# Two-layer gated attention and feed-forward on one core: second norm's transposes moved ahead of the second score pair, first values moved up, layer 1's norm scale and offset behind the transposes

## Chip, cores and metric

One core of a Trainium2 chip runs the kernel. The metric is device microseconds for one execution. All arithmetic is fp32; where a product needs more than one pass of rounded operands, it is split into a high and a low part.

## What is computed

The batch has 8 sequences of 256 tokens, 256 wide. Each of two layers adds a gated cross attention (16 heads, 77 context rows) and a gated feed-forward. Layer 0's feed-forward has 8 experts by position; layer 1's has one shared expert and 7 routed ones with room for 732 tokens each. Only layer 1's second norm has a scale and an offset (`ln_g`, `ln_b`).

```python
x = x + tanh(g_xattn[0]) * attention0(layernorm(x), ctx)
x = x + tanh(g_ffn[0])   * experts_by_position(layernorm(x))
x = x + tanh(g_xattn[1]) * attention1(layernorm(x), ctx)
h = layernorm(x) * ln_g + ln_b
logits = h @ Wr                       # top 2 of 7 experts
x = x + tanh(g_ffn[1])   * (routed(h, logits) + silu(h @ W1s) * (h @ W3s) @ W2s)
```

## The kernel before

It is written by hand for each engine; every engine runs its own instruction list in order, and semaphores join them. There are four stages: attention of layer 0 (to about 150 us), layer 0's experts (to 250), attention of layer 1 (to about 400), and the shared and routed experts of layer 1.

Attention runs one batch element per step, `attention_step` in each engine's block, software-pipelined over three steps. The heads are four units u = 0..3: units 0 and 1 are the first half of the columns (dt 0) for both halves of the rows, units 2 and 3 the second (dt 1). In step g TensorE (PE) computes the scores of g (`scores`, L562, two pairs), transposes the probabilities (`prob_transposes`, L573), multiplies with the values of g-1 (`weighted_values`, L582, dt 0 and dt 1), transposes the attention output of g-2 (`out_transposes`, L523 from `o_q`), projects it (`project_out`, L594), transposes the first norm of g+1 (`norm_t`, L523 from `xn`), makes its queries (`queries`, L602), and transposes the second norm of g-3 (`norm2_t`, L523 from `xn2`, which the profile also prints as `xn`). In layer 1 it adds the router's logits of g-3 (`route_logits`, L551).

PSUM sets the order. `bank[0]` takes, one after the other, the second norm's, the output's and the first norm's transposes and the queries; each must be copied out by ScalarE (ACT) before the next is written: `norm2_t` copies to `stage` (L982), `out_t` to `o_t` (L1012, two instructions), `norm_t` to `xn_t` (L975), `queries` to `q_t` (L991). `bank[1]` takes values, projection and, in its last columns, the logits. VectorE (DVE) takes the maxima and subtracts them (`max_sub`), normalises the values (`normalise_out`, L1345 and L1347), adds the projection to the residual (`add_attention`, L1355), and makes both norms; GpSimd (POOL) makes the reciprocal roots and the low parts. In layer 1 the second norm is made in two DVE steps, `centre2` (L1312, with `ln_g`) and `norm2` (L1326, with `ln_b`), from full rows of scale and offset.

SyncE (SP) issues all loads. Per step it places the values of one batch element on the block diagonal tile `v_blk`, 8 small DMAs for each half (`place_values`, L335). Half dt of g is placed once `weighted_values(g-1, dt)` has read the old contents:

```python
if not isinstance(g, int) or g > 0:
    sp.wait_ge(pv_psum, KT * g - KT + 1 + dt)
```

In layer 0 a step also zeroes a part of two tensors in device memory (L344, L345).

In the routed experts PE transposes the next expert's rows in the middle and at the end of an expert (`slots_t`, L874); ACT copies them to the high part (`slots_hi`, L1221), DVE makes the low part (`slots_lo`, L1593).

## Time and profile before

| | us |
|---|---|
| median of 3 runs | 887.07 (884.72 to 891.02) |
| the profiled execution | 888.85 |
| its span, first to last instruction | 887.10 |
| PE busy | 851.7 (96% of the span) |
| DVE, ACT, POOL busy | 525.6, 427.2, 275.7 |
| mean granted TensorE clock | 0.981 of full |

Span and durations come from the one profiled execution. Its time stands 1.75 us above its span and 1.78 us above the median. A busy PE is not a PE at its peak, since matmuls overlap; how long a piece takes is read from the start of one to the start of the next. Rows that print x20 for ten products count both passes of an fp32 product.

### The profile page before, as it was taken

Reading aid. Unit: us, or ns where it says so; the run is one execution under the profiler, and the core shown is the slowest. Engines: PE = TensorE matmul, PEld = TensorE weight load, DVE = VectorE, ACT = ScalarE, POOL = GpSimd, SP = SyncE. Lnnn points to the kernel's source line nnn. Section 1 sums busy time; section 2 is a strip of 40 time slices with the busy share of each in tenths; the row PEclk is TensorE's granted clock in tenths of the full one; section 3 lists DMA queues with packets and bytes.
Section 4 is the critical chain, followed back from the end, with each engine's and each line's share of the span. In section 5 each row is a group of like instructions: output and inputs, shape, how many; then the busy total and the mean of one; then the engine's idle time right before and its main releaser. Section 6 shows DMA issues by size and latency. Waiting matters only on the chain.

```text
span 887.1 us, 18253 instructions
## 1 busy us (share of the span) xinstructions
PE 851.7 (96%) x6116; PEld 799.5 (90%) x6116; DVE 525.6 (59%) x1128; ACT 427.2 (48%) x939; POOL 275.7 (31%) x328
## 2 busy tenths in 40 slices
PE   8899989999969999999999999999999999999997
PEld 6788878999948888879898999999999999999986
DVE  4677744555567887647336573636556473645648
ACT  3556654777736665632324462615345361525431
POOL 5244314877754443135552002020100102020130
PEclk9999989999969999999999999999999999999999
DMA  5242327766530000020213323413233131422152
GB/s 204 66 132 95 124 67 278 219 218 211 180 101 5 8 6 6 8 96 19 70 45 98 104 74 84 125 40 108 80 95 86 64 106 52 130 74 96 62 185 101
DMA packets 74841, 86.98 MB, mean 98 GB/s; under 512 B 31188, under 2 KB 46962, under 8 KB 74668
## 3 DMA queue, kind: packets, MB, share of 16 engines
q1 hardware_dynamic: 70956, 79.86, 29.3%
q0 software_dynamic: 3552, 6.55, 2.2%
q8 instruction: 24, 0.39, 0.2%
q14 instruction: 21, 0.17, 0.1%
q10 hardware_dynamic: 288, 0.01, 0.0%
HBM read 64.08 MB, written 23.63 MB: 99 GB/s over the span
## 4 chain that ended last, share of the span: by engine, by line
PE 80%; SPq 9%; DVE 4%; issue 3%; ACT 2%; DMA 1%; POOL 0%; DVEq 0%; ACTq 0%; POOLq 0%
PE score L274 14%; PE score L276 14%; PE score L275 13%; SPq L335 8%; PE bank_p L274 7%; PE bank_p L275 7%; PE bank_p L276 7%; PE bank L582 5%; PE bank L594 2%; PE bank L602 2%; PE bank_p L573 2%; PE bank L523 2%; PE bank L874 1%; PE score L562 1%; DVE residual L1734 1%
## 5 line engine op out<-in xcount | busy, mean ns | idle before, releaser
L1135 ACT ACTIVATE silu<-score 128x366 f32<-128x366 f32 (+1 forms) x144 | 72.6, 504 | 278.5 <-PE score L276 278.5
L1494 DVE TENSOR_TENSOR prod<-silu,score 128x366 f32<-128x366 f32 (+1 forms) x144 | 82.1, 570 | 114.8 <-ACT silu L1135 112.5
L274 PE MATMUL score<-xe_hi,w_hi 128*128 128x366 f32 x448 | 149.3, 333 | 0.0
L276 PE MATMUL score<-xe_hi,w_lo 128*128 128x366 f32 x448 | 148.3, 331 | 0.0
L275 PE MATMUL score<-xe_lo,w_hi 128*128 128x366 f32 x448 | 148.2, 331 | 0.0
L1979 POOL DMA_INDIRECT slots_out<-yh,home_of x42 | 40.8, 972 | 336.7 <-DVE yh L1621 336.7
L274 PE MATMUL bank_p<-w_hi,hid_hi 128*122 128x256 f32 (+1 forms) x448 | 127.3, 284 | 0.7 <-DVE hid_lo L1502 0.5
L275 PE MATMUL bank_p<-w_lo,hid_hi 128*122 128x256 f32 (+1 forms) x448 | 125.7, 281 | 0.0
L276 PE MATMUL bank_p<-w_hi,hid_lo 128*122 128x256 f32 (+1 forms) x448 | 125.6, 280 | 0.0
L1805 POOL TENSOR_TENSOR w_lo<-raw,w_hi 128x512 fp32r<-128x512 f32 x62 | 82.6, 1363 | 31.3 <-ACT w_hi L949 24.3
L582 PE MATMUL bank<-v_blk,prob_t 128*128 128x136 f32 x640 | 84.4, 290 | 5.6 <-DMA v_blk<-values 5.2
L274 PE MATMUL score<-act_hi,w_hi 128*128 (+2 forms) x256 | 86.8, 339 | 0.0
L582 PEld LDWEIGHTS bank<-v_blk,prob_t 128*128 128x128 f32 x640 | 80.3, 198 | 6.8 <-issue 6.1
L276 PE MATMUL score<-act_hi,w_lo 128*128 (+2 forms) x256 | 86.1, 336 | 0.0
L275 PE MATMUL score<-act_lo,w_hi 128*128 (+2 forms) x256 | 85.9, 336 | 0.0
L274 PEld LDWEIGHTS score<-xe_hi,w_hi 128*128 128x128 f32 x448 | 84.6, 189 | 0.2 <-issue 0.2
L276 PEld LDWEIGHTS score<-xe_hi,w_lo 128*128 128x128 f32 x448 | 84.7, 189 | 0.0
L275 PEld LDWEIGHTS score<-xe_lo,w_hi 128*128 128x128 f32 x448 | 84.6, 189 | 0.0
L274 PEld LDWEIGHTS bank_p<-w_hi,hid_hi 128*122 128x122 f32 (+1 forms) x448 | 82.6, 184 | 1.7 <-DVE hid_lo L1502 0.9
L275 PEld LDWEIGHTS bank_p<-w_lo,hid_hi 128*122 128x122 f32 (+1 forms) x448 | 82.7, 185 | 0.1
L276 PEld LDWEIGHTS bank_p<-w_hi,hid_lo 128*122 128x122 f32 (+1 forms) x448 | 82.7, 185 | 0.0
L1502 DVE TENSOR_TENSOR hid_lo<-prod,hid_hi 128x366 fp32r<-128x366 f32 (+1 forms) x136 | 76.2, 560 | 0.5 <-ACT hid_hi L1185 0.3
(208 smaller groups left out, 1723.0 us busy)
## 6 DMA issues: line engine op xcount, KB each, us to landing
raw<-w_second_d SPq DMA_DIRECT2D x108, 256.0 KB, 2.7
raw<-w_first_d SPq DMA_DIRECT2D x72, 256.0 KB, 3.1
slot_rows<-yh SPq DMA_DIRECT2D x8, 771.0 KB, 3.4
yh<-slot_rows SPq DMA_DIRECT2D x8, 674.6 KB
v_blk<-values SPq DMA_DIRECT2D x256, 5.0 KB, 2.0
slots_out<-yh SPq DMA_DIRECT2D x8, 512.0 KB, 4.3
wa<-attn_w_d SPq DMA_DIRECT2D x8, 256.0 KB, 4.2
yh<-slots_out SPq DMA_DIRECT2D x4, 512.0 KB, 7.9
```

The source lines that it names most:

```text
L274: nc.tensor.matmul(o, a_hi, b_hi, start=start, stop=False)
L275: nc.tensor.matmul(o, a_hi, b_lo, start=False, stop=False)
L276: return nc.tensor.matmul(o, a_lo, b_hi, start=False, stop=stop)
L335: sp.dma_start(v_blk[h:P:HT, dt * PT:(dt + 1) * PT, h * HD:(h + 1) * HD], v_g[:, at:at + HD].rearrange("(t k) d -> k t d", t=PT)).then_inc ...
L523: last = nc.tensor.transpose(o[:, kt * S + h * P:kt * S + (h + 1) * P], src[:, h, kt * P:(kt + 1) * P], ident[:])
L573: last = nc.tensor.transpose(bank_p[grp][:, i * P:(i + 1) * P], prob[u][:, j * P:(j + 1) * P], ident[:])
L582: last = nc.tensor.matmul(bank[1][:, qt * VW:(qt + 1) * VW], prob_t[:, dt * PT + j, qt * P:(qt + 1) * P], v_blk[:, dt * PT + j, :], start= ...
L1135: nc.scalar.activation(silu[0:rows_n, buf, 0:width], src, ACT.Silu).then_inc(silu_done, 1)
L1494: nc.vector.tensor_tensor(prod[0:rows_n, buf, 0:width], silu[0:rows_n, buf, 0:width], up, ALU.mult).then_inc(gu_free, 1)
L1502: nc.vector.tensor_tensor(lo, prod[0:rows_n, buf, 0:hi.shape[-1]], hi.bitcast(F32), ALU.subtract).then_inc(hid_ready, 1)
L1805: return nc.gpsimd.tensor_tensor(w_lo[:, at, :], raw[:, slot_f, :], w_hi[:, at, :].bitcast(F32), ALU.subtract)
L1979: nc.gpsimd.indirect_dma_start(out=ye, out_offset=bass.IndirectOffsetOnAxis(ap=home_of[:, e, j:j + 1], axis=0), in_=y_out[:, j, :], in_off ...
```

## The change

In the attention steps of both layers PE now issues `weighted_values(g-1, 0)` right behind the transposes of unit 2, and `out_transposes(g-2)` behind those values instead of ahead of them. `norm2_t(g-3)` stood between the first score pair and the probability transposes; it now stands behind the projection, ahead of the second score pair. The logits of layer 1 are computed behind the last probability transposes of the step, ahead of the second values. ACT's copies, DVE's `normalise_out` and POOL's `act_low` are put in the matching order; DVE's first `normalise_out` now also waits for the output transposes of the step.

In layer 1 the second norm is the plain one in one DVE step. Scale and offset are applied by ACT when it copies the transposed norm out of PSUM, from a column of each (`ln_cols`, loaded by four DMAs of 4 bytes per partition), in two instructions instead of one. The rows that are kept for the routed experts are without scale and offset, so `slots_hi` first writes scaled rows to `xe_rows` and then copies them to the high part: four instructions instead of two.

```diff
@@ -394,9 +400,13 @@
             sp.dma_start(xs[:, HALVES:2 * HALVES, :], x[:, HALVES:2 * HALVES, :]).then_inc(x_second, 16)
-            sp.dma_start(row[:], rows).then_inc(rows_in, 16)
+            sp.dma_start(row[:], rows[:, 0:2, :]).then_inc(rows_in, 16)
             sp.dma_start(rw[:], router_w).then_inc(rows_in, 16)
             sp.dma_start(xs[:, 2 * HALVES:, :], x[:, 2 * HALVES:, :]).then_inc(x_rest, 16)
+            for i in range(2):
+                for kt in range(KT):
+                    sp.dma_start(ln_cols[:, i, kt:kt + 1],
+                                 rows[0, 2 + i, kt * P:(kt + 1) * P].rearrange("(p o) -> p o", o=1)).then_inc(ln_in, 16)
             attention_loads(0)
@@ -623,21 +633,15 @@
                 scores(g, par, 1, start)
-                if three:
-                    norm2_t(g - 3)
                 if some:
                     prob_transposes(g - 1, 2)
-                if two:
-                    if three:
-                        pe.wait_ge(stage_ready, staged(layer, g - 3))
-                    out_transposes(g - 2)
-                if layer == 1 and three:
-                    route_logits(g - 3, bank[1][:, HALVES * VW:])
-                if some:
                     if layer == 0 and n == 1:
                         pe.wait_ge(v_ready, 3)
+                    if two:
+                        pe.wait_ge(oq_ready, KT * g - KT)
                     weighted_values(g - 1, 0)
-
+                if two:
+                    out_transposes(g - 2)
                 if some:
@@ -658,18 +662,24 @@
                     pe.wait_ge(oq_ready, KT * g - 1)
-                if layer == 1 and three:
-                    pe.wait_ge(logit_done, b - 2)
                 if two:
                     project_out(g - 2, bank[1])
+                if three:
+                    if not final_step:
+                        pe.wait_ge(xnt_ready, g + 2)
+                    norm2_t(g - 3)

                 scores(g, par, 2, start)
                 scores(g, par, 3, start)
                 prob_transposes(g, 0)
+                if three:
+                    pe.wait_ge(stage_ready, staged(layer, g - 3))
                 if some and not final_step:
                     queries(g + 1)
                 if final_step:
                     pe.wait_ge(x_new, g - 1)
+                    if layer == 1:
+                        route_logits(g - 3, bank[1][:, HALVES * VW:])
                     weighted_values(g - 1, 1)
@@ -679,6 +689,8 @@
                         pe.wait_ge(x_new, g - 1)
+                    if layer == 1 and three:
+                        route_logits(g - 3, bank[1][:, HALVES * VW:])
                     weighted_values(g - 1, 1)
@@ -974,12 +986,18 @@

-            def norm2_t(g, first):
+            def norm2_t(layer, g, first):
                 act.wait_ge(xn2t_psum, g + 1)
                 if not first:
                     act.wait_ge(lo_ready, g)
                     act.wait_ge(hi_ready, g)
-                nc.scalar.activation(stage[:].rearrange("p k s -> p (k s)"), bank[0][:], ACT.Copy).then_inc(stage_ready, 1)
+                if layer == 0:
+                    last = nc.scalar.activation(stage[:].rearrange("p k s -> p (k s)"), bank[0][:], ACT.Copy)
+                else:
+                    for kt in range(KT):
+                        last = nc.scalar.activation(stage[:, kt, :], bank[0][:, kt * S:(kt + 1) * S], ACT.Identity,
+                                                    scale=ln_cols[:, 0, kt:kt + 1], bias=ln_cols[:, 1, kt:kt + 1])
+                last.then_inc(stage_ready, 1)

@@ -1026,15 +1044,12 @@
                 final_step = n == B - 1
-                if three:
-                    norm2_t(g - 3, layer == 0 and n == 3)
-                    high(layer, g - 3, b - 3)
                 if some:
                     probs_t(g - 1, 2)
+                    exps(g, 0)
                 if two:
                     out_t(layer, g - 2)
                 if some:
-                    exps(g, 0)
                     probs_t(g - 1, 3)
@@ -1048,7 +1063,11 @@
                     keep_rows(b - 3, g - 3)
+                if three:
+                    norm2_t(layer, g - 3, layer == 0 and n == 3)
                 probs_t(g, 0)
+                if three:
+                    high(layer, g - 3, b - 3)
                 if layer == 1 and n in (0, 1):
@@ -1216,9 +1235,14 @@
             def slots_hi(e, hf):
+                part = slice(hf * HC, (hf + 1) * HC)
                 for kt in range(KT):
                     act.wait_ge(xet_psum, 4 * e + KT * hf + kt + 1)
-                    nc.scalar.activation(xe_hi[:, kt, hf * HC:(hf + 1) * HC], bank[kt][:, 0:HC], ACT.Copy).then_inc(xe_hi_done, 1)
+                    nc.scalar.activation(xe_rows[:, kt, :], bank[kt][:, 0:HC], ACT.Identity,
+                                         scale=ln_cols[:, 0, kt:kt + 1], bias=ln_cols[:, 1, kt:kt + 1]).then_inc(xe_scaled, 1)
+                for kt in range(KT):
+                    act.wait_ge(xe_scaled, 4 * e + KT * hf + kt + 1)
+                    nc.scalar.activation(xe_hi[:, kt, part], xe_rows[:, kt, :], ACT.Copy).then_inc(xe_hi_done, 1)

@@ -1302,30 +1326,12 @@

-            def centre2(b, g):
-
-                dve.wait_ge(xn2t_psum, g)
-                if not (isinstance(b, int) and b == 0):
+            def norm2(layer, b, g, first):
+                if not first:
+                    dve.wait_ge(xn2t_psum, g)
+                if layer == 1 and not (isinstance(b, int) and b == 0):
                     dve.wait_ge(rows_kept, b)
-                dve.wait_ge(mv2_done, g + 1)
-                for h in range(HALVES):
-                    last = nc.vector.scalar_tensor_tensor(out=xn2[:, h, :], in0=xs_row(b, h), scalar=mv2[:, h, 0:1], in1=row[:, 2, :],
-                                                          op0=ALU.subtract, op1=ALU.mult)
-                last.then_inc(h_step, 1)
-
-            def norm2(layer, b, g, first):
-                if layer == 0:
-                    if not first:
-                        dve.wait_ge(xn2t_psum, g)
-                    normalise(lambda h: xs_row(b, h), xn2, mv2, rstd2, rstd2_done, xn2_ready, g)
-                    return
-
-                dve.wait_ge(rstd2_done, g + 1)
-                dve.wait_ge(h_step, b + 1)
-                for h in range(HALVES):
-                    last = nc.vector.scalar_tensor_tensor(out=xn2[:, h, :], in0=xn2[:, h, :], scalar=rstd2[:, h:h + 1], in1=row[:, 3, :],
-                                                          op0=ALU.mult, op1=ALU.add)
-                last.then_inc(xn2_ready, 1)
+                normalise(lambda h: xs_row(b, h), xn2, mv2, rstd2, rstd2_done, xn2_ready, g)

@@ -1344,6 +1350,8 @@
                 dve.wait_ge(recip_done, KT * g + dt + 1)
+                if dt == 0 and not (isinstance(g, int) and g == 0):
+                    dve.wait_ge(ot_psum, g)
                 nc.vector.tensor_tensor(o_q[:, :, dt * P:(dt + 1) * P].rearrange("p q (h d) -> p q h d", d=HD),
@@ -1385,11 +1392,9 @@
                 max_sub(g, 0, start)
-                max_sub(g, 1, start)
                 if some:
                     normalise_out(g - 1, 0)
-                if layer == 1 and three:
-                    keep_logits(b - 3, bank[1][:, HALVES * VW:])
+                max_sub(g, 1, start)
                 if start:
@@ -1399,16 +1404,20 @@
                 if final_step:
-                    normalise_out(g - 1, 1)
+                    last_half(layer, b, g, three)
                 max_sub(g, 3, start)
-                if layer == 1 and two:
-                    centre2(b - 2, g - 2)
                 if two:
                     norm2(layer, b - 2, g - 2, layer == 0 and n == 2)
                 if ahead:
                     norm(layer, b + 2, False)
                 if some and not final_step:
-                    normalise_out(g - 1, 1)
+                    last_half(layer, b, g, three)
+
+            def last_half(layer, b, g, three):
+                if layer == 1 and three:
+                    dve.wait_ge(pv_psum, KT * g)
+                    keep_logits(b - 3, bank[1][:, HALVES * VW:])
+                normalise_out(g - 1, 1)

@@ -1457,6 +1466,8 @@
                     normalise_out(g, 1)
+                    dve.wait_ge(ln_in, 16 * 2 * KT)
+                    nc.vector.tensor_scalar(ln_cols[:, 0, :], ln_cols[:, 0, :], (1.0 + EPS) ** -0.5, None, ALU.mult)
                     for t in hid0_hi + hid0_lo:
@@ -1590,8 +1598,9 @@
                     dve.wait_ge(xe_hi_done, 4 * e + KT * hf + kt + 1)
-                    nc.vector.tensor_tensor(xe_lo[:, kt, hf * HC:(hf + 1) * HC], bank[kt][:, 0:HC],
-                                            xe_hi[:, kt, hf * HC:(hf + 1) * HC].bitcast(F32), ALU.subtract).then_inc(xe_ready, 1)
+                    part = slice(hf * HC, (hf + 1) * HC)
+                    nc.vector.tensor_tensor(xe_lo[:, kt, part], xe_rows[:, kt, :],
+                                            xe_hi[:, kt, part].bitcast(F32), ALU.subtract).then_inc(xe_ready, 1)

@@ -1815,14 +1824,14 @@
                     add_out_bias(layer, b + 1)
-                if three:
-                    act_low(b - 3, g - 3)
                 if layer == 1 and (n is None or n < B - 3):
                     add_first_layer(b + 3)
                 if ahead:
                     rstd_of(mv, rstd, eps_done, rstd_done, g + 2, mv_done)
                 if two:
                     rstd2_of(layer, g - 2)
+                if three:
+                    act_low(b - 3, g - 3)

```

The rest of the diff reserves the tiles, renames a semaphore, passes `layer` to `norm2_t` and drops the calls of `centre2` behind the loop and the scaling of `row[:, 2]`.

PE, a step of layer 1's loop, before (names: `xn2` second norm, `o_q` attention output, `prob2` and `prob3` units 2 and 3, `xn` first norm):

```order
L562 MATMUL score<-kb_85,q_t_82 128x154 x8
...
L523 MATMUL bank0<-ident_56,xn2_97 128x128 x4
...
L573 MATMUL bank_p1<-ident_56,prob2_76 128x128 x2
...
L523 MATMUL bank0<-ident_56,o_q_100 128x128 x4
L551 MATMUL bank1<-rw_68,stage_98 128x8 x4
...
L582 MATMUL bank1<-v_blk_78,prob_t_84 128x136 x10
...
L573 MATMUL bank_p1<-ident_56,prob3_77 128x128 x2
...
L523 MATMUL bank0<-ident_56,xn_80 128x128 x4
...
L594 MATMUL bank1<-wa_110,o_t_99 128x256 x4
```

The same stretch of PE after:

```order
L572 MATMUL score<-kb_86,q_t_83 128x154 x8
...
L583 MATMUL bank_p1<-ident_56,prob2_77 128x128 x2
...
L592 MATMUL bank1<-v_blk_79,prob_t_85 128x136 x10
...
L533 MATMUL bank0<-ident_56,o_q_101 128x128 x4
...
L583 MATMUL bank_p1<-ident_56,prob3_78 128x128 x2
...
L533 MATMUL bank0<-ident_56,xn_81 128x128 x4
...
L604 MATMUL bank1<-wa_111,o_t_100 128x256 x4
L533 MATMUL bank0<-ident_56,xn2_98 128x128 x4
```

Between the transposes of `o_q` and those of `xn`, both into bank 0, there now stands only one piece, the transposes of unit 3; before, the logits and ten value products stood there too.

ACT at the first expert's rows, ahead of the experts' loop, before:

```order
L1221 ACTIVATE xe_hi_111<-bank0 128x366
L1221 ACTIVATE xe_hi_111<-bank1 128x366
L1221 ACTIVATE xe_hi_111<-bank0 128x366
L1221 ACTIVATE xe_hi_111<-bank1 128x366
L1255 UNCONDITIONAL_BRANCH
```

The same place of ACT after:

```order
L1241 ACTIVATE xe_rows_130<-bank0,ln_cols_65 128x366
L1241 ACTIVATE xe_rows_130<-bank1,ln_cols_65 128x366
L1245 ACTIVATE xe_hi_112<-xe_rows_130 128x366 x2
L1241 ACTIVATE xe_rows_130<-bank0,ln_cols_65 128x366
L1241 ACTIVATE xe_rows_130<-bank1,ln_cols_65 128x366
```

Both scaled copies now stand ahead of the first copy to the high part.

## Rows read from the trace of the kernel before

**Rows 1.** PE in a step of layer 1's loop: start us, us, engine, line, operation, [idle before].
```profile
311.43 0.81 PE L562 MATMUL score<-kb,q_t 32*128 32x154 f32 x16
312.49 0.66 PE L523 MATMUL bank<-ident,xn 128*128 128x128 f32 x4 [0.26 <-DVE xn L1326]
312.98 0.71 PE L573 MATMUL bank_p<-ident,prob 128*128 128x128 f32 x5
314.04 0.65 PE L523 MATMUL bank<-ident,o_q 128*128 128x128 f32 x4 [0.35 <-ACT stage L982]
...
317.75 0.71 PE L573 MATMUL bank_p<-ident,prob 128*128 128x128 f32 x5
318.29 0.60 PE L523 MATMUL bank<-ident,xn 128*128 128x128 f32 x4
318.90 1.97 PE L594 MATMUL bank<-wa,o_t 128*128 128x256 f32 x8
320.80 0.81 PE L562 MATMUL score<-kb,q_t 32*128 32x154 f32 x16
321.53 0.76 PE L573 MATMUL bank_p<-ident,prob 128*128 128x128 f32 x5
322.13 1.89 PE L602 MATMUL bank<-xn_t,wa 128*128 128x256 f32 x8
...
324.41 2.48 PE L582 MATMUL bank<-v_blk,prob_t 128*128 128x136 f32 x20
326.82 0.81 PE L562 MATMUL score<-kb,q_t 32*128 32x154 f32 x16
```

**Rows 2.** Timeline of PE, two score pieces one step apart, layer 0.
```profile
97.52 0.81 PE L562 MATMUL score<-kb,q_t 32*128 32x154 f32 x16
...
111.57 0.81 PE L562 MATMUL score<-kb,q_t 32*128 32x154 f32 x16
```

**Rows 3.** Timeline of all engines, out transposes to projection, end of layer 0.
```profile
140.36 0.63 PE L523 MATMUL bank<-ident,o_q 128*128 128x128 f32 x4
...
141.03 0.84 ACT L1012 ACTIVATE o_t<-bank,bias_cols 128x256 f32<-128x256 f32 x2 [2.59 <-PE bank L523]
...
141.92 0.48 PE L594 MATMUL bank<-wa,o_t 128*128 128x256 f32 x1
```

**Rows 4.** Timeline of SP's queue in layer 0, a step and the next one's start.
```profile
92.39 12.32 SPq L335 DMA_DIRECT2D v_blk<-values  x16
...
106.39 0.60 SPq L335 DMA_DIRECT2D v_blk<-values  x1
```

**Rows 5.** Chain of waits in layer 0, start us, us, what.
```profile
52.40 2.33 PE bank L582 x20
...
54.75 0.66 SPq L335
...
98.97 0.56 SPq L335
```

**Rows 6.** Timeline of PE, the last batch's first values in layer 0.
```profile
128.24 4.87 PE L582 MATMUL bank<-v_blk,prob_t 128*128 128x136 f32 x20 [2.31 <-DMA v_blk<-values]
```

**Rows 7.** Windows: us, busy (count) of PE, PEld, DVE, ACT, POOL, then granted clock, DMA share, GB/s.
```profile
128.00:132.00 4.00, 3.76 (x17) 3.79 (x17) 0.00 (x0) 0.61 (x2) 0.00 (x0) 0.50 0.08 11
```

**Rows 8.** Groups by line, shapes apart, ACT: count, busy us, mean ns, idle before.
```profile
L982 ACT ACTIVATE stage<-bank 128x512 f32<-128x512 f32 x15 | 9.0, 599 | 21.0 <-PE bank L523 21.0
...
L1164 ACT ACTIVATE y_rows<-bank_p,tanh_gate 128x256 f32<-128x256 f32 x7 | 3.3, 475 | 11.9 <-PE bank_p L276 11.8
...
L1020 ACT ACTIVATE v_rows<-bank 128x256 f32<-128x256 f32 x4 | 1.4, 382 | 2.3 <-PE bank L610 2.3
```

**Rows 9.** Timeline of PE, layer 1's last logits.
```profile
398.75 1.06 PE L551 MATMUL bank<-rw,stage 128*128 128x8 f32 x8 [0.69 <-ACT stage L982]
```

**Rows 10.** Timeline of PE, the first expert's second transposes.
```profile
492.71 0.89 PE L874 MATMUL bank<-ident,yh 122*128 122x122 f32 x6 [0.92 <-DVE xe_lo L1593]
```

**Rows 11.** Timeline of ACT in the first expert, the silu behind the slot copies.
```profile
522.83 0.48 ACT L1135 ACTIVATE silu<-score 128x366 f32<-128x366 f32 x1 [0.54 <-PE score L276]
```

More of the change, by code:

```diff
@@ L95, in flamingo_program @@
         neg_half, eps_tile, eps_twice = halves_of[:, 0], halves_of[:, 1], halves_of[:, 2]
-        row = sb("row", [P, 4, D])
+        row = sb("row", [P, 2, D])
+        ln_cols = sb("ln_cols", [P, 2, KT])
         bias_cols = sb("bias_cols", [P, 2, 3, KT])
@@ L163, in flamingo_program @@
         xe_lo = sb("xe_lo", [P, KT, CAP], F32R)
+        routing = place[0]
         eq = sb("eq", [P, T, E1])
@@ L181, in flamingo_program @@
         end_ffn = place[0]
+        place[0] = routing
+        xe_rows = sb("xe_rows", [P, KT, HC])
+        assert place[0] <= end_routing
         yh_rows = yh[:].rearrange("p t n -> p (t n)")
@@ L1108, in attention @@
                     values(1, 0, banks[5])
-                norm2_t(g - 2, False)
+                norm2_t(layer, g - 2, False)
                 high(layer, g - 2, B - 3)
@@ L1116, in attention @@
                     keep_rows(B - 2, g - 1)
-                norm2_t(g - 1, False)
+                norm2_t(layer, g - 1, False)
                 high(layer, g - 1, B - 2)
@@ L1128, in attention @@
                     keep_rows(B - 1, g)
-                    norm2_t(g, False)
+                    norm2_t(layer, g, False)
                     high(layer, g, B - 1)
@@ L1376, in scale_rows @@
                 last.then_inc(bias_done, 1)
-                nc.vector.tensor_scalar(row[:, 2, :], row[:, 2, :], (1.0 + EPS) ** -0.5, None, ALU.mult)
             def attention_step(layer, b, n):
@@ L1468, in attention @@
                     norm2_stats(B - 2, g - 1, False)
-                if layer == 1:
-                    centre2(B - 2, g - 1)
                 norm2(layer, B - 2, g - 1, False)
@@ L1477, in attention @@
                     keep_logits(B - 2, bank[0])
-                    centre2(B - 1, g)
                 norm2(layer, B - 1, g, False)
```

3 lines of the change are left out of this document (2 added, 1 removed).

## The prediction

> **What bounds the kernel now.** I read the windows first, to see where PE idles: hardly anywhere in the experts, so the attention stages are where this change can pay. Then I read PE's timeline for one step of each layer, from the start of one piece to the start of the next. In layer 1's loop a step takes 326.82 - 311.43 = 15.39 us [rows 1]. Three waits stand in it. The second norm's transposes start 1.06 us behind the first scores, where the same scores take 0.73 (320.80 to 321.53): 0.33 of waiting for DVE's norm. From the transposes of unit 2 to those of the output it is again 1.06 us, where five transposes take 0.54 (317.75 to 318.29): 0.52 of waiting until ACT has copied `stage`. From the first norm's transposes to the projection it is 0.61, where four transposes take 0.49: 0.12. Together 0.97 us; without them PE would need 14.42.
>
> Layer 0 is another case. PE's step is 111.57 - 97.52 = 14.05 us [rows 2], but SP's queue needs 106.39 - 92.39 = 14.00 us for its 16 placements and two zeroing stores [rows 4]. The chain of waits shows them locked together: in step 2 the second half's placement starts at 54.75, 0.02 us behind the end of the second values (52.40 + 2.33) [rows 5], and from there the chain is issue time of the queue up to the last batch's first values at 128.24, where PE has waited 2.31 us for the landing [rows 6]. PE cannot gain in layer 0 by its own order; it can only lose the queue's start.
>
> **The change, part by part.** The sum is made on the profiled execution (888.85) and carried over to the median as a difference.
>
> 1. The new wait in every step with output transposes, both layers. They write bank 0, ACT copies them with two instructions, and then the first norm's transposes (in the last step the projection) may start. At the end of layer 0 this path stands free of other work: transposes 140.36, copy 141.03 for 0.84, PE goes on at 141.92 [rows 3]: 1.56 us. Behind them PE now has only their own 0.49 and the 0.54 of unit 3's transposes [rows 1]. So it waits 1.56 - 1.03 = 0.53 us. Before, ten value products (2.41, from 324.41 to 326.82) covered this. Bounds: 0, if all of it were covered, and 1.56, if nothing were. I take 0.53, the row of the same path.
>
> 2. The scale and offset in ACT's copy (layer 1). The copy of `stage` is 0.60 us now [rows 8]. The new one is a pair like that of `o_t`, 0.84 [rows 3], with one more column operand each. One such operand costs 475 - 382 = 93 ns [rows 8], so 0.84 + 0.19 = 1.03. The path from norm 2's transposes to the next writer of bank 0 was 1.55 (312.49 to 314.04); it becomes 1.55 - 0.60 + 1.03 = 1.98. PE now has four transposes, scores and five transposes to do meanwhile: 0.49 + 0.73 + 0.60 = 1.82 [rows 1]. It waits 0.16 us, bounds 0 and 0.6. In layer 0 the copy stays single and is covered. The Trainium skill, "ScalarE: Activation LUTs", section "What ACT_TABLE_LOAD costs", gives about 93 ns for each pointer operand but lets neighbouring instructions overlap by as much; by it the pair may be about 0.1 us shorter and the 0.16 nearly vanish.
>
> 3. Layer 1's steps: -0.97 + 0.53 + 0.16 = -0.28, four times in the loop: -1.1. Step 2 has output transposes but no second norm yet, so it only gains a wait: +0.5. The last step I take like one of the loop: -0.3. Together -0.9 us.
>
> 4. Layer 0's steps. Inside a step the old 0.52 goes and 0.53 comes: nothing. In step 2 the old wait did not exist, and the output transposes, which before lay in PE's wait for the placement, now stand behind the first values. The second values end 0.49 + 0.53 = 1.02 us later, the queue's second half starts behind them [rows 5], and all later placements with it. In the loop the queue's ninth issue came at 98.97, 1.45 us behind the end of the second values at 97.52 [rows 2, 5]. Between first and second values there are now 0.49 (output), 0.53 (wait) and 0.49 (second norm) more, 1.51: the slack is gone, and each of four steps adds 0.06 to 0.1 us. The last batch's first values so come at 128.24 + 1.3.
>
> 5. What that does to the clock. Behind the 2.31 us wait those values ran at a granted clock of 0.50, the 1.2 GHz level [rows 7], and took 4.87 us instead of 2.48 [rows 1, 6]. In the last step PE now carries the two transposes and the new wait, 1.5 us, and reaches this point later, while the landing is 1.3 us later; the transposes of unit 3 overlap, so I put the remaining wait at about 1.4 us. If the clock holds over it, 2.4 us come back: layer 0 ends at 1.3 - 2.4 = -1.1. If it falls all the same, layer 0 ends at +1.3.
>
> The Trainium skill, "TensorE: Matmul & The Clock Gate", section "Part 4: PE-mode transpose", says that transposes do not count as a busy PE. By that rule the moved pieces make a run of transposes with a wait in it that could lower the clock. The nearest row is against a loss in the steps: from the end of the scores (311.43 + 0.73) to the end of the output transposes (314.04 + 0.49) stood only transposes and waits, 2.4 us, and the products behind them ran at full pace [rows 1]; the new run is 0.49 + 0.54 + 0.53 + 0.49, 2.1 us.
>
> 6. Tail of layer 1. The last logits wait 0.69 us for `stage` [rows 9]; with part 2's copy 0.43 more. `centre2` goes (two DVE instructions), but DVE was ahead there.
>
> 7. Routed experts. The first rows are exposed: PE's second transposes waited 0.92 us for `xe_lo` [rows 10]. Two scaled copies now stand ahead of the first high copy; each is a 366-wide instruction of 0.48 [rows 11] plus two column operands, 0.67, overlapping: +1.15 us. Inside the experts the four extra instructions of each of 7 rounds delay a `silu`. ACT idled 0.54 us before it [rows 11], so it is about 0.6 late; PE fills two tiles ahead, so I take 0.03 per expert, 0.2 in all, bounds 0 and 4.
>
> 8. Loads. Four small DMAs come ahead of `place_values`, where SP then waits for the first values anyway; the rows' load is halved. Zero, bounds -0.3 and +1. POOL's `act_low` moves behind a root that waits for DVE; nobody needs it before the next step. Zero.
>
> Sum: -1.1 (layer 0) - 0.9 (layer 1) + 0.4 + 1.15 + 0.2 = -0.2 us. On the profiled execution 888.65, on the median 886.9.
>
> **Rivals.**
> - The clock still falls at the end of layer 0. Then layer 0 is +1.3 instead of -1.1: 889.3. For it: PE does only transposes for some microseconds there, as before. Against: the wait is shorter by 0.9.
> - The new wait is covered after all (ACT or DVE order kinder than I think). Then 10 or 11 steps lose 0.53 less; in layer 0 the queue's start still binds, so 0.5 there plus 3 us in layer 1: 883.4. Against: rows 3 show the bare path.
> - Slower: ACT is late. In the new order ACT must do the exponential of unit 0 before it may copy `o_t`. From the end of the first scores to the copy of `o_t` PE's order leaves 0.54 + 2.41 + 0.67, 3.6 us [rows 1, 3]. From the point where DVE's two instructions for unit 0 and ACT's exponential together take longer than that, because DVE comes late from the second values, each microsecond goes to every step, in layer 0 through the queue too. With 0.9 us in 11 steps: 886.9 + 9.9 = 896.8. Against it: DVE is rid of two instructions per step in layer 1. The like in the experts (0.6 us of PE wait in each of 7) would give 891.
> - Slower by far: by the transpose rule the clock falls in each step. Each values piece of 2.4 us more in 10 steps: 911.
> - The change does not do what it says: the `stage` wait stays. I see no way, since bank 0's next writer stands 1.8 us behind.
>
> **How the numbers follow.** Forecast 0.50, clock falls 0.20, covered 0.10, ACT late or experts 0.17, clock falls in each step 0.03. A measurement of this kernel can tell a change of about 1% (8.9 us) from none. The first three and half of the fourth stay within 1%. The range takes 881.5 (the covered case and less queue time) to 893.5 (half of the ACT case); outside are 2 in 10. Faster by over 1%: 0.05, what the bounds leave below 878. Slower by over 1%: 0.10, from the ACT case's upper half and the clock.
>
> **What would show it.** Right: in layer 1's loop a step near 15.1 us, a wait of PE before the first norm's transposes for `o_t` of about 0.3 to 0.5 us, none before the second norm's; layer 0's step near 14.1, the last batch's first values near 129.5; the gap before the first expert about 1.1 us longer; a span within 3 us of 887. Wrong: a loop step of 14.5 or of 16, a queue that starts step 2's second half at 54.75 as before, or waits of PE for ACT inside the experts.

## The result and the profile after

The changed kernel takes 891.6 us (median of 20 runs, 885.4 to 896.8), the kernel before 887.0 beside it (20 runs, 884.7 to 891.0): ratio 1.0045, 95% interval 1.0028 to 1.0063. It is slower by 4.6 us where I had forecast 0.2 us less. That is within 1% and inside my range, but on the wrong side, and the interval leaves no doubt of the sign.

Each run also gives TensorE's mean granted clock. The 20 runs of the changed kernel lie on a line, from 885.4 us at 0.993 to 896.8 us at 0.980; the kernel before does the same (883.7 at 0.993, 892.1 at 0.980 in a later session). So I read each kernel twice: by its median, and at equal clock, with every run moved along one line of time over clock (540 us per 1.0 of clock, fitted to all runs of the study). The mean of 12 runs is good to some 0.3 us, and the kernel before alone moves by 0.6 us between sessions (880.1 to 880.7 us with its line extended to 1.000). At equal clock the changed kernel stands 3.4 us above the kernel before. The rest of its 4.6 is clock.

This second reading has two limits. A line of its own would fall by 480 us per 1.0 of clock for the kernel before and by 725 for the changed one, so the 3.4 holds near the means of both (about 0.987; the own lines give 3.2 there) and says nothing of a clock of 1.000. And the mean clock is in part made by the kernel's own waits, so equal clock takes out a part of what a wait costs.

The profiled execution took 895.9 us (span 894.1, clock 0.980), against 888.9 (887.1, 0.981), so it shows 7 us and not 4.6. Where they come in, by PE's timeline: +0.5 at the first values of step 1 (42.13 us), +2.6 at those of step 3, +1.7 at the start of layer 0's experts, +2.3 at layer 1's first transposes, +5.5 at its step 3, +4.1 at the last logits, +5.7 at the first sums of the routing, +8.1 at the second expert's rows, +7.0 at the end. The loss is made in four places, and layer 1's loop gives some back. These are lags between two single executions; how far they can be trusted is taken up below, under "Why the prediction was wrong".

PE's timeline of one step of layer 1's loop, which answers to [rows 1] (start us, us, engine, line, operation, idle before):
```profile
316.79 0.81 PE L572 MATMUL score<-kb,q_t 32*128 32x154 f32 x16
317.52 0.77 PE L583 MATMUL bank_p<-ident,prob 128*128 128x128 f32 x5
318.12 2.48 PE L592 MATMUL bank<-v_blk,prob_t 128*128 128x136 f32 x20
320.44 0.60 PE L533 MATMUL bank<-ident,o_q 128*128 128x128 f32 x4
320.88 0.71 PE L583 MATMUL bank_p<-ident,prob 128*128 128x128 f32 x5
322.05 0.65 PE L533 MATMUL bank<-ident,xn 128*128 128x128 f32 x4 [0.46 <-ACT o_t L1030]
322.54 1.89 PE L604 MATMUL bank<-wa,o_t 128*128 128x256 f32 x8
324.26 0.60 PE L533 MATMUL bank<-ident,xn 128*128 128x128 f32 x4
324.79 0.81 PE L572 MATMUL score<-kb,q_t 32*128 32x154 f32 x16
...
331.79 0.81 PE L572 MATMUL score<-kb,q_t 32*128 32x154 f32 x16
```
The step is 331.79 - 316.79 = 15.00 us instead of 15.39. The three old waits are gone, one new one stands where it was forecast (0.46 for `o_t`), and the wait for `stage` of 0.16 that I had added did not come.

Step 1 of layer 1, first PE, then VectorE (same columns):
```profile
274.37 1.41 PE L572 MATMUL score<-kb,q_t 32*128 32x154 f32 x16 [0.96 <-DVE prob L1344]
275.71 1.33 PE L583 MATMUL bank_p<-ident,prob 128*128 128x128 f32 x5
276.83 2.95 PE L592 MATMUL bank<-v_blk,prob_t 128*128 128x136 f32 x20
279.62 0.71 PE L583 MATMUL bank_p<-ident,prob 128*128 128x128 f32 x5
280.16 0.60 PE L533 MATMUL bank<-ident,xn 128*128 128x128 f32 x4
282.22 0.81 PE L572 MATMUL score<-kb,q_t 32*128 32x154 f32 x16 [1.46 <-DVE prob L1344]
```
```profile
276.67 0.80 DVE L1344 TENSOR_TENSOR prob<-score,mx 128x616 f32<-128x616 f32 x1
279.82 0.26 DVE L1351 RECIPROCAL recip<-bank 128x16 f32<-128x16 f32 x1 [2.35 <-PE bank L592]
280.11 0.42 DVE L1355 TENSOR_TENSOR o_q<-bank,recip 128x256 f32<-128x256 f32 x1
280.45 0.79 DVE L1340 TENSOR_REDUCE mx<-score 128x8 f32<-128x616 f32 x1
281.27 0.80 DVE L1344 TENSOR_TENSOR prob<-score,mx 128x616 f32<-128x616 f32 x1
```
This is what the prediction never looked at. `normalise_out` now stands between the two `max_sub` of the first pair. VectorE idles 2.35 us for the first values, though unit 1's scores have long been there; unit 1's subtraction therefore ends at 282.07, and PE's scores of unit 2, which wait for it, stand 1.46 us. From step 2 on PE has output transposes and a projection to do meanwhile, and nothing waits. Layer 0's step 1 has the same wait (1.46 us); there PE stands for late values right behind it. The 0.96 us at the start of step 1 is another matter: `ones_last` and `five` below have the old order in step 1 and wait 0.96 us there too, behind the same scores at the low clock (1.41 instead of 0.81 us).

The last logits, answering to [rows 9], and PE behind them:
```profile
402.89 1.06 PE L561 MATMUL bank<-rw,stage 128*128 128x8 f32 x8 [1.11 <-ACT stage L998]
403.81 0.56 PE L280 MATMUL score<-act_hi,w_hi 128*128 128x512 f32 x1
404.16 0.63 PE L281 MATMUL score<-act_lo,w_hi 128*128 128x512 f32 x1
...
407.14 0.55 PE L282 MATMUL score<-act_hi,w_lo 128*128 128x512 f32 x1
407.54 0.39 PE L280 MATMUL score<-act_hi,w_hi 128*128 128x512 f32 x1
```
The wait grew from 0.69 to 1.11 us, as forecast. Behind it the same products take 0.63 us for a stretch and then 0.39 again. The clock granted is 0.83 on average over 398 to 408 us, where it was 1.00 before: the stretch lies at the 1.2 GHz level. From the last logits to the first sums it is 10.8 us, before 9.2.

The first expert's rows, answering to [rows 10], and ScalarE's copies there:
```profile
499.73 1.45 PE L886 MATMUL bank<-ident,yh 122*128 122x122 f32 x6 [2.05 <-DVE xe_lo L1602]
```
```profile
497.41 1.20 ACT L1241 ACTIVATE xe_rows<-bank,ln_cols 128x366 f32<-128x366 f32 x2 [10.28 <-PE bank L886]
498.51 0.90 ACT L1245 ACTIVATE xe_hi<-xe_rows 128x366 fp32r<-128x366 f32 x2
```
2.05 - 0.92 = 1.13 us more, forecast 1.15. The transposes behind it take 1.45 instead of 0.89 us, the granted clock is low soon after, and 1.1 us more were lost before the second expert's rows:
```profile
501.00:504.00 3.00, 3.00 (x14) 0.66 0.02 5
```
(window in us, its length, PE's busy time and count, granted clock, DMA share, GB/s; the same window before shows 1.00.) In the seven profiles with this wait of 2.05 us, four lost 1.2 to 1.7 us behind it and three nothing. `five`, whose waits there are shorter (below, under "The first expert"), lost 1.7 us too, so the length of the wait alone does not decide it.

### The profile page after: what moved, and what is told of

The parts are those of the page before. It is cut to its first block, busy times and chain, and to the rows that moved or that the text cites. A ratio compares the mean times of both kernels' runs of the same rounds, so it can differ in the third digit from the quotient of the medians.

```text
span 894.1 us, 18320 instructions
## 1 busy us (share of the span) xinstructions
PE 852.8 (95%) x6116; PEld 801.0 (90%) x6116; DVE 521.1 (58%) x1112; ACT 451.7 (51%) x979; POOL 276.4 (31%) x328
## 4 chain that ended last, share of the span: by engine, by line
PE 86%; SPq 5%; DVE 3%; ACT 2%; issue 2%; DMA 1%; POOL 0%; DVEq 0%; ACTq 0%; POOLq 0%
PE score L281 13%; PE score L280 13%; PE score L282 13%; PE bank L592 7%; PE bank_p L280 7%; PE bank_p L281 7%; PE bank_p L282 7%; SPq L341 4%; PE bank L612 3%; PE bank_p L583 2%; PE bank L604 2%; PE score L572 2%; PE bank L533 2%; PE bank L886 1%; DVE residual L1743 1%
```

## The experiments

**Halves of the change.** `order_only` has the new order of all engines, and the scale and offset as rows on VectorE as before. `cols_only` has the old order, and the scale and offset as columns.

> The kernel before with the reordering alone: PE's, ScalarE's, VectorE's and POOL's steps in the new order, layer 1's norm scale and offset as rows on VectorE as before (centre2 and norm2), no small loads, expert rows rounded straight from PSUM. Theory 1 (the loss is made by the order: the start of each layer, above all VectorE's order in step 1 of layer 1, and the values that arrive late; the scale part adds only 0.5 us at the first values and 1.1 at the first expert): about 1.6 us below the changed kernel, 890 us, scores 2 of layer 1's step 1 still wait 1.4 us for VectorE. Theory 2 (the loss is made by the scale and offset): 886 to 887 us, as the kernel before. Layer 1's loop step: 15.0 us if the order shortened it, 15.4 if the removed centring did.

> The kernel before with the scale and offset part alone: columns loaded by four small DMAs, layer 1's stage copy in two scaled halves, VectorE without centring, expert rows scaled and then rounded; the order of every step as before. Theory 1: +0.5 us at the first values, +1.1 at the first expert, and up to 0.4 per step of layer 1 because here PE's output transposes wait for a stage copy that is 0.43 us longer: 888.5 to 891 us. If that wait is covered (VectorE's shorter step brings the normed rows earlier): 888.5. Theory 2 (the whole loss of 4.6 us is made here): 891.5 us with layer 1's loop step at 15.4 or above.

Measured: `order_only` 889.2 us, ratio 1.0028 (1.0009 to 1.0047); `cols_only` 891.4, ratio 1.0044 (1.0021 to 1.0067). Each half is slower than the kernel before by itself; at equal clock they stand 3.1 and 3.3 us above it, the whole change 3.4. So they don't add, and the loop accounts for most of that. In `order_only` a step of layer 1's loop takes 344.10 - 328.68 = 15.42 us, in `cols_only` about 15.5, with both 15.00, where before has 15.39. Over four steps the halves lose some 0.5 us and the pair gains 1.6: 2.1 of the 3.0 us that are missing from the sum. The 0.39 us gained per step belongs to the pair: with the new order but VectorE still centring (1.38 us per step, the row below, and 0.94 for its second instruction), its normalised output comes late and PE's values wait for it, 0.23 us.
```profile
326.57 1.38 DVE L1315 SCALAR_TENSOR_TENSOR xn<-residual,mv,row 128x256 f32<-128x256 f32 x2
```
My expectation named 15.0 us if the order shortened the loop and 15.4 if the removed centring did; `order_only` gave 15.42 and `cols_only` 15.5, so neither does it alone. Step 1 tells the halves apart. `order_only` has the wait for VectorE, as I expected; `cols_only`, with the old order, has none at the same place:
```profile
277.88 0.81 PE L562 MATMUL score<-kb,q_t 32*128 32x154 f32 x16 [1.45 <-DVE prob L1341]
```
```profile
276.33 0.81 PE L572 MATMUL score<-kb,q_t 32*128 32x154 f32 x16
```
`cols_only` showed the low stretch behind the last logits too (10.8 us), with the old order around it.

**VectorE's order in step 1 alone.**
```diff
                 max_sub(g, 0, start)
+                if n == 1:
+                    max_sub(g, 1, start)
                 if some:
                     normalise_out(g - 1, 0)
-                max_sub(g, 1, start)
+                if not (n == 1):
+                    max_sub(g, 1, start)
```


> The changed kernel with VectorE's old order in step 1 of each layer alone: both max_sub of the first pair before normalise_out(g-1, 0). Theory 1 (VectorE's second max_sub waits there for the first weighted values and PE's third score for it): scores 2 of layer 1's step 1 start without their 1.46 us of wait, step 2 of layer 1 is reached about 2.4 us earlier than in the changed kernel, time 889.2 us. Theory 2 (another wait takes its place, the second values or the clock): 891.6 us, no change. Both: later steps keep their length of 15.0 us.

Measured 889.6 us, 2.0 below the changed kernel; ratio 1.0047 (1.0029 to 1.0066), in a session where the kernel before stood at 886.2. At equal clock 1.9 us less than the changed kernel. PE of this kernel at the same place:
```profile
278.87 0.60 PE L533 MATMUL bank<-ident,xn 128*128 128x128 f32 x4
279.40 0.81 PE L572 MATMUL score<-kb,q_t 32*128 32x154 f32 x16
280.13 0.76 PE L583 MATMUL bank_p<-ident,prob 128*128 128x128 f32 x5
```
The wait is gone. The ratios of the two kernels are the same, so by them nothing is gained; the trace says 1.5 us and the comparison at equal clock 1.9. The mechanism is shown; its price is not clear of noise by the ratios.

**The small loads.** `ln_late` issues them behind all loads of layer 0's attention:
```diff
-            for i in range(2):
...
             attention_loads(0)
+            for i in range(2):
...
```


> The changed kernel with the four small loads of the scale and offset issued after all loads of layer 0's attention instead of ahead of the values. Theory 1 (they hold the values' first stores and loads up by 1.8 us, of which 0.46 reach PE): weighted values of step 1 at 41.7 us instead of 42.1, time 891.1 us. Theory 2 (they cost nothing, since the values wait for something else): 891.6 us, step 1 as before. Theory 3 (the delay also makes the late values of step 3): weighted values of step 3 wait 1.5 us instead of 2.33, time 890.3 us.

Measured 900.2 us, ratio 1.0158: all three theories failed, since none asked who reads them. VectorE scales the columns at the end of layer 0, and waited there, with the last norms behind it:
```profile
147.41 0.17 DVE L1470 TENSOR_SCALAR ln_cols<-ln_cols 128x2 f32<-128x2 f32 x1 [7.47 <-DMA ln_cols<-rows_d]
```
`ln_ffn` issues them inside layer 0's experts and scales them at layer 1's start.

> The changed kernel with the four small loads issued inside layer 0's expert layer and the column scaling done by VectorE at the start of layer 1, where nothing waits for it. Theory 1 (the loads cost layer 0 more than the 0.46 us at the first values, since the values stay late down to step 3: its first weighted values stood at 74.5 us in the changed kernel, at 72.7 with the order alone): step 3 back at 72.7 us, about 1.6 us less in all, 890.0 us. Theory 2 (the late values of step 3 are made by the order): 891.1 to 891.6 us. Theory 3 (as when the loads were put behind attention's loads: something waits for them again): 892 us or more, with a wait named ln_cols in the profile.

Measured 892.5 us, ratio 1.0051 (1.0030 to 1.0072), at equal clock the same as the changed kernel within 0.1 us. Theory 2: the loads cost nothing that can be measured. Step 3's first values did stand at 73.5 us instead of 74.5, but in `slots_early` below, whose loads are where the changed kernel has them, they stood at 73.2.

**Layer 0 in its old order** (all four engines), layer 1 in the new.

> The changed kernel with the order of the kernel before in all steps of layer 0 (PE, ScalarE, VectorE, POOL), the new order in layer 1 alone. Theory 1 (the new order gains nothing in layer 0, whose step of 14.1 us is the same either way, and costs its start some 1.7 us): expert layer 0 begins 1.7 us earlier than in the changed kernel (152.6 us there at two low stretches of the clock), 890.0 us, or 1.7 us less at equal clock. Theory 2 (layer 0's loss is made by the small loads ahead of the values alone): no change, 891.6 us.

Measured 891.0 us, ratio 1.0034 (1.0017 to 1.0050), at equal clock 1.0 us below the changed kernel. The expert layer began at 151.6 us, 1.0 earlier and not 1.7. By these numbers layer 0's new order costs about 1 us and gives nothing; the interval of the ratio overlaps the changed kernel's.

**The last logits' wait covered.** The two halves of the shared expert's last piece ahead of the logits are taken apart, and the norm's transposes go between them:
```diff
                 for gu in range(2):
+                    if gu == 1 and between is not None:
+                        between()
...
-                    shared_gate_up(0, 3)
...
+                    shared_gate_up(0, 3, last_norm2_t)
```


> The changed kernel with layer 1's last norm transposes put between the two halves of the shared expert's piece 3, so that six products cover the last stage copy. Theory 1 (the wait of 1.11 us for that copy is followed by a stretch at the low clock, 8 products of 0.63 instead of 0.39 us, in all four kernels that have it and in neither that waits 0.69): wait gone, no low stretch, from the last logits to the first sums 9.2 us instead of 10.8, in all 2.7 us less: 888.9 us. Theory 2 (the clock falls there by its own course): only the 1.1 us of wait, 890.5 us, and the products behind it still take 0.63 us.

Measured 889.3 us, ratio 1.0023 (1.0006 to 1.0040), 2.3 below the changed kernel by the median, 1.5 at equal clock. From the last logits to the first sums it is 9.1 us. PE waits nowhere and runs at full clock:
```profile
396.16 0.60 PE L533 MATMUL bank<-ident,xn 128*128 128x128 f32 x4
396.51 0.48 PE L280 MATMUL score<-act_hi,w_hi 128*128 128x512 f32 x1
...
397.99 0.95 PE L561 MATMUL bank<-rw,stage 128*128 128x8 f32 x8
398.80 0.48 PE L280 MATMUL score<-act_hi,w_hi 128*128 128x512 f32 x1
399.12 0.39 PE L281 MATMUL score<-act_lo,w_hi 128*128 128x512 f32 x1
```

**Is it the wait's length?** Four kernels are the kernel before with nothing but the last stage copy made longer: in three plain pieces (`split_last`), in two halves with a scale column of ones (`ones_last`), in two halves with scale and bias columns (`dose_two`), and so with the second half in two pieces (`dose_three`).

> The kernel before with one edit: layer 1's last stage copy, a single plain copy of 512 columns, is made in three pieces (256, 128 and 128 columns), so that the last logits wait about 1.1 us instead of 0.69; nothing else differs. Theory 1 (the length of this wait decides whether the clock goes low behind it): a low stretch from 400 us on, 8 products of 0.63 us, 10.8 us from the last logits to the first sums, in all 2.0 us above the kernel before. Theory 2 (the low stretch there belongs to the changed kernel's other timing): 9.2 us as before, in all 0.4 us above.

> The kernel before with layer 1's last stage copy alone in the changed kernel's form: two halves of 256 columns, each scaled by a column (of ones here, so that nothing computed changes). In three plain pieces it waited 0.81 us and no low stretch followed. This form should wait 1.11 us as in the changed kernel. Theory 1 (the last logits' wait, once it is 1.11 us, is followed by the low clock, as in the six kernels that have it): 10.8 us from the last logits to the first sums instead of 9.2, in all 2.0 us above the kernel before, ratio 1.002. Theory 2 (the low clock there needs the changed kernel's other timing as well): 9.2 us, and 0.4 us above the kernel before, ratio 1.0005.

> The kernel before with layer 1's last stage copy in two halves that take both a scale column (ones) and a bias column (the norm's epsilon, so that the last batch's normed rows are larger by it). With the scale column alone the copy took 0.84 us, the wait was 0.93 us, and no low stretch followed; with both it should be 1.02 and 1.11 us, as in the changed kernel. Theory 1 (a wait of 1.11 us at this place is followed by the low clock): 10.8 us from the last logits to the first sums, ratio to the kernel before 1.002. Theory 2 (not the wait but the changed kernel's other timing): 9.2 us, ratio 1.0005.

> As the kernel with two halves and both columns, but with the second half cut in two pieces of 128 columns, for a wait of about 1.3 us. Theory 1: the low clock follows here too, 10.8 us or more from the last logits to the first sums, ratio 1.0025. Theory 2: 9.2 us, ratio 1.0007.

```
kernel       copy  wait  profiled: logits to sums   ratio to before (95%)
split_last   0.72  0.81   9.2, full clock           1.0003 (0.9984 to 1.0021)
ones_last    0.84  0.93   9.2, full clock           1.0020 (0.9998 to 1.0041)
dose_two     1.02  1.11   9.2, full clock           1.0032 (1.0016 to 1.0049)
dose_three   1.26  1.35  10.8, low stretch          1.0026 (1.0008 to 1.0044)
```
With a wait that is longer by 0.42 us and nothing else changed, `dose_two` stands at 1.0032, 2.8 us; the lower end of its interval is 1.4 us. At equal clock the four stand 0.2, 0.2, 1.3 and 1.8 us above the kernel before. So in `dose_two` and `dose_three` the longer wait costs more than itself, and theory 2's 1.0005 lies outside `dose_two`'s interval. Where `dose_two` loses it is not shown: its profiled execution, the fastest of its 12 (885.2 us against a median of 888.9), has the wait of 1.11 us and no low stretch:
```profile
395.10 1.06 PE L551 MATMUL bank<-rw,stage 128*128 128x8 f32 x8 [1.11 <-ACT stage L1133]
396.01 0.48 PE L274 MATMUL score<-act_hi,w_hi 128*128 128x512 f32 x1
396.33 0.39 PE L275 MATMUL score<-act_lo,w_hi 128*128 128x512 f32 x1
```
`dose_three`, 1.35 us:
```profile
397.40 1.18 PE L551 MATMUL bank<-rw,stage 128*128 128x8 f32 x8 [1.35 <-ACT stage L1133]
398.44 0.77 PE L274 MATMUL score<-act_hi,w_hi 128*128 128x512 f32 x1
399.01 0.63 PE L275 MATMUL score<-act_lo,w_hi 128*128 128x512 f32 x1
```
Over all profiled executions: waits up to 0.93 us, none of four with a low stretch; 1.11 us, seven of eight; 1.35, one of one. The seven all have the scaled copies of the changed kernel in every step; of the kernels that differ from before in this wait alone there is one execution each, low at 1.35 us and not at 1.11. That the wait brings the low stretch is therefore likely and not shown, and that it is not certain to is shown. What else it hangs on stays open.

**The first expert.** The second half's transposes wait for the scaled copy and no longer for the low halves; ScalarE's scaled copies wait for the low halves in their place (two lines, not shown).
```diff
-                        pe.wait_ge(xe_ready, n - KT + 1)
+                        pe.wait_ge(xe_scaled, n - KT + 1)
```


> The changed kernel with the second half of each expert's row transposes waiting for the scaled copy alone and no longer for the low halves, ScalarE keeping the copy back instead. Theory 1 (the transposes of 0.89 us go into the wait of 2.05 us): 0.9 us less at the first expert, 890.7 us. Theory 2 (the wait of 2.05 us in one piece is also what the low clock behind it follows, 1.1 us between the first and second expert in the changed kernel's profile): up to 2.0 us less, 889.6 us. Theory 3 (ScalarE's new wait delays its silus): the experts take over 50.44 us each and nothing is gained.

Measured 891.8 us, ratio 1.0032 (1.0009 to 1.0055), 0.3 us less at equal clock, no more than its noise. The wait of 2.05 became two:
```profile
496.87 0.99 PE L886 MATMUL bank<-ident,yh 122*128 122x122 f32 x6 [0.53 <-ACT xe_rows L1243]
499.04 0.43 PE L280 MATMUL score<-xe_hi,w_hi 128*128 128x366 f32 x1 [1.18 <-DVE xe_lo L1604]
```
0.53 + 1.18 = 1.71. My 0.9 was wrong: the transposes had waited only for the first low half, and already lay beside the second.

**Together.** `all_four` takes VectorE's order, the loads, the covered copy and the early transposes; `five` also layer 0's old order.

> The changed kernel with four edits together: VectorE's old order in step 1, the small loads inside layer 0's expert layer, the covered last stage copy, the early slot transposes. If the losses found so far are all of them and add (2.0 measured for step 1, 1.6 for the loads, 2.7 for the last copy, 0.9 at the first expert): 7.2 us below the changed kernel, 884.4 us, some 2 us below the kernel before. If they overlap (the clock gives the same microsecond only once): 886 to 887 us, as the kernel before.

> The four edits together (VectorE's old order in step 1, small loads in layer 0's expert layer, covered last stage copy, early slot transposes) and layer 0 in its old order. They stood at the kernel before's time with layer 0 in the new order (ratio 1.0009). Theory 1 (layer 0's order costs 1.7 us): ratio 0.999, 886.5 us where before has 887.5. Theory 2 (it costs nothing): ratio 1.001. The clock decides more than either: with two or three low stretches in the profile 882 us, with nine 889 us.

Measured 888.8 us, ratio 1.0009 (0.9987 to 1.0031), and 885.7 us, ratio 0.9988 (0.9968 to 1.0008). At equal clock `all_four` stands 3.4 us below the changed kernel and `five` 4.7. The single edits give 1.9 - 0.1 (loads) + 1.5 + 0.3 = 3.6 and, with layer 0's 1.0, 4.6 there; such a sum is good to about 1 us. By the ratios no single edit is clear of the changed kernel's interval (1.0028 to 1.0063), and `all_four` overlaps its edge; `five` lies wholly below it. So the five places together hold the loss, with shares that are each uncertain. With these five undone, what is left of the change is worth 1.4 us at equal clock against the kernel before; by the median it can't be told from none.

## Why the prediction was wrong

Two steps of the sum failed: layer 1's steps 0 and 1 were left out of it (point 3), and the 2.4 us that the clock was to give back in layer 0 were not there to be given back (point 5). The numbers below follow the prediction's points.

1. The new wait for `o_t`: forecast 0.53, measured 0.46. Right.
2. ScalarE's scaled stage copy: forecast 1.03 us, measured 1.02. Right, by the price of a column operand that [rows 8] gave. I had thought that the overlap of neighbours by about 93 ns, which the Trainium skill, "ScalarE: Activation LUTs", section "What ACT_TABLE_LOAD costs", gives beside its 93 ns for each pointer operand, might take 0.1 us off this. The trace agrees with the page and not with my reading of it: two copies of 0.564 us (their mean) take 1.02, an overlap of 0.11, but [rows 3]'s 0.84 had it in it already. The 0.16 us of wait behind it did not come.
3. Layer 1's steps: forecast -0.28 in the loop, measured -0.39; +0.5 in step 2, measured +0.5 (PE's lag behind the kernel before grew from 4.96 us at its first scores, 283.29 to 288.25, to 5.47 at step 3's, 296.31 to 301.78). **The step that failed is the list of steps itself.** I priced step 2, the loop and the last step, and passed over steps 0 and 1, because PE's order hardly changes there. VectorE's does, and PE waited 1.46 us for it in step 1 (and 0.96 at its start, behind scores that ran at the low clock). From layer 1's first transposes to step 2 the lag grew from 2.27 to 4.96 us, where I had booked nothing. Of these 2.7 us the order makes 1.46; the 0.96 comes with the low clock and not with the order. `dve_step1` gives 1.9 us back.
4. The queue in layer 0: I took 1.3 us at the last batch's first values; between the two profiled executions it was 2.9, and step 3's first values waited 2.33 us for their landing. But four more kernels of this study (`split_last`, `ones_last`, `dose_two`, `dose_three`) have before's code up to 390 us. Their profiles put these values at 129.66 to 130.25 us, and only before's own at 128.24; the mean of the five is 129.6. The changed kernel's code up to there was profiled three times (with `slots_early` and `tail_cover`), mean 130.7. The means are 1.2 us apart, so the 1.3 was about right, and the excess in 2.9 is the spread between executions.
5. The clock at the end of layer 0: forecast to hold, with 2.4 us given back. The wait was 1.37 us as I had put it (1.4), but the values behind it still took 4.17 us. **This term failed, and in its premise.** I read the 4.87 us that it was to shorten from one execution. In the four other profiles of the same code the values took 2.56 us already, so there was nothing to give back:
```profile
131.11 4.17 PE L592 MATMUL bank<-v_blk,prob_t 128*128 128x136 f32 x20 [1.37 <-DMA v_blk<-values]
```
```profile
129.79 2.56 PE L582 MATMUL bank<-v_blk,prob_t 128*128 128x136 f32 x20 [1.85 <-DMA v_blk<-values]
```
(the first in the changed kernel, the second in `split_last`.) Nor does the wait's length decide it: the values ran at full clock behind 1.19, 1.62 and 1.85 us, and at the low clock behind 1.22, 1.29 and 1.39. Without the term the sum is +2.2 us. The expert layer of layer 0 began 1.5 us later by the means of the five and the three profiles, where I had -1.1. My first rival, 889.3, came nearer, in part by luck: in `tail_cover`, the same code up to there, the clock held.
6. The tail of layer 1: forecast +0.43, measured +0.42 for the wait, and 1.6 us more for the low stretch behind it. I had weighed the clock only where it was already low, not where a wait grew.
7. The first expert: forecast +1.15, measured +1.13. Inside the experts I took +0.2 in all, bounds 0 and 4; measured was a gain: 50.44 us for each instead of 50.60, with PE waiting nowhere in either. The whole scale part makes it (`cols_only` 50.43, `order_only` 50.60; in `cols_only` the products of `xe_hi` and `w_hi` take 331 ns on average, before and in `order_only` 333). Why was not tried.
8. Loads at zero: `ln_ffn` agrees, to within its noise of some 0.3 us.

The rivals: "ACT is late" and "the clock falls in each step" did not happen; the loop kept full clock through its run of transposes. So against point 5 of the prediction, the rule on transposes in the Trainium skill, "TensorE: Matmul & The Clock Gate", section "Part 4: PE-mode transpose", made no low stretch in any step of layer 1's loop. On the profiled execution I forecast -0.2 us and it was +7.0. By the lags of PE, measured less forecast: 2.8 at the end of layer 0 (1.7 against -1.1), 0.6 in its experts, 2.7 in steps 0 and 1 of layer 1, -0.3 over the other steps and the last wait, 1.6 by the clock behind the last logits, 1.1 by a low stretch behind the first expert's rows, -1.3 in the experts: 7.2 in all. At the median, 4.8 us off, the shares can't be read off. Between executions of one code PE's place moves more than most of these terms: layer 1's step 3 stands at 292.2 to 296.4 us in the five profiles of before's code, mean 294.7, and at 298.1 to 301.8 in the changed kernel's three, mean 300.1. The difference of the means is 5.5 us, and 2.9 of it come in steps 0 and 1, so layer 1's part holds; layer 0's is corrected in points 4 and 5.

## What to carry to other kernels

When an order is changed on several engines, write down each step that the program writes out by hand, the first ones above all, and ask on every engine what the moved instruction now holds up: an instruction that waits, moved ahead of one that is ready, is harmless only where the consumer has other work. A wait of PE that grows by 0.4 us can cost 2 us through the clock behind it, so price a growing wait with the low clock and look for work to put over it. And where times lie on a line over the granted clock, compare kernels at equal clock as well, or a schedule's gain drowns in it. Before a low stretch is booked as a gain, look for it in a second execution: one that stands in a single profile may not be in the next.

## What I had not expected of the hardware

- At the same place and with the same wait of 1.11 us the clock went low in seven profiled executions and stayed up in one. The low stretch there cost 1.6 us each time (10.8 us against 9.2).
- At the end of layer 0 the same code ran its values at the low clock in one profiled execution (4.87 us) and at full clock in four (2.56 us).
- The time of this kernel follows the mean granted clock over 11 us (885.4 to 896.8), more than the whole change is worth.
